# Attention's second product: four split fp32r products an image, or fp32 products of two images in four column groups

## The reference, cut to what matters

```
qkv = x @ qkv_w + qkv_b
attn = einsum('bqd,bkd->bqk', q * scale, k)
rel_h = einsum('bhwc,hkc->bhwk', q, Rh);  rel_w = einsum('bhwc,wkc->bhwk', q, Rw)
attn = softmax(attn + rel_h[..., :, None] + rel_w[..., None, :], axis=-1)
out = einsum('bqk,bkd->bqd', attn, v)
y = out @ proj_w + proj_b
```

## Time and profile before

| | |
|---|---|
| median of the runs | 1782.19 us |
| the profiled execution: its time, its span | 1781.53 us, 1779.3 us |
| PE busy, weight loads busy | 1477.8 us (83%), 1308.6 us |
| DVE, ACT, POOL busy | 1251.0, 899.5, 800.3 us |
| mean granted clock of TensorE | 0.798 |
| DMA, mean over the span | 92 GB/s |

### The profile page before, as it was taken

The page is one execution under the profiler, slowest core; times in us unless marked ns, Lnnn a source line. Parts: engine busy times, 40 slices in busy tenths (PEclk is TensorE's granted clock), DMA queues, the critical chain, the costliest instruction groups (busy, mean ns, idle before and its releaser), DMA issues. The chain is left out here.

```text
span 1779.3 us, 50706 instructions
## 1 busy us (share of the span) xinstructions
PE 1477.8 (83%) x19315; PEld 1308.6 (74%) x19315; DVE 1251.0 (70%) x4156; ACT 899.5 (51%) x1894; POOL 800.3 (45%) x888
## 2 busy tenths in 40 slices
PE   4868888888876886989976989899998697888977
PEld 4757777777765685878965667688884587787976
DVE  7877877877878656878856694544446646887874
ACT  3633333333345665767833433555553555666862
POOL 2812222222226054758952210556651415676974
PEclk9955555555558898999987589999995689999998
DMA  3000000000002585658415304333225458666812
GB/s 88 1 21 4 4 4 4 4 4 4 4 4 84 152 241 150 154 138 172 96 37 160 126 14 148 114 96 93 87 78 154 145 149 266 162 140 145 162 31 58
DMA packets 71882, 164.52 MB, mean 92 GB/s; under 512 B 17842, under 2 KB 43066, under 8 KB 69148
## 3 DMA queue, kind: packets, MB, share of 16 engines
q1 hardware_dynamic: 66268, 148.44, 31.6%
q0 software_dynamic: 5376, 12.85, 2.4%
HBM read 93.84 MB, written 67.42 MB: 91 GB/s over the span
## 5 line engine op out<-in xcount | busy, mean ns | idle before, releaser
L1065 POOL TENSOR_TENSOR l_arena<-l_arena,l_arena 98x784 fp32r<-98x784 f32 x192 | 360.5, 1881 | 136.5 <-ACT l_arena L1303 132.0
L514 PE MATMUL gru_ps_r<-gru_hp,gru_wp 128*128 128x16 f16 x3920 | 199.7, 176 | 68.3 <-DVE gru_hp L489 68.3
L514 PEld LDWEIGHTS gru_ps_r<-gru_hp,gru_wp 128*128 128x128 f16 x3920 | 150.4, 105 | 88.7 <-DVE gru_hp L489 88.7
L1300 ACT ACTIVATE l_arena<-l_ps 98x784 fp32r<-98x784 f32 x192 | 158.6, 826 | 103.7 <-PE l_ps L1154 101.7
L1375 DVE TENSOR_REDUCE l_mt<-l_ps 98x4 fp32r<-98x784 f32 x192 | 186.8, 973 | 27.4 <-PE l_ps L1133 22.9
L514 PE MATMUL gru_ps_n<-gru_hp,gru_wp 128*128 128x16 f16 x3920 | 191.2, 174 | 0.0
L567 POOL TENSOR_TENSOR gru_kept<-gru_keep,l0s_state 128x32 f32<-128x32 f32 x196 | 49.3, 252 | 305.9 <-ACT gru_keep L582 305.9
L1171 PE MATMUL l_ps<-l_arena,l_arena 128*66 128x196 f32 x768 | 162.7, 264 | 22.3 <-DVE l_arena L1343 20.7
L580 ACT ACTIVATE gru_reset<-gru_ps_r,gru_unscale 128x32 f32<-128x32 f32 x196 | 56.5, 288 | 216.9 <-PE gru_ps_r L514 216.9
L1172 PE MATMUL l_ps<-l_arena,l_arena 128*66 128x196 f32 x768 | 158.9, 259 | 0.0
L1303 ACT ACTIVATE l_arena<-l_ps 98x784 f32<-98x784 f32 x192 | 157.2, 819 | 0.0
(11 more groups left out here) (386 smaller groups left out, 4512.9 us busy)
## 6 DMA issues: line engine op xcount, KB each, us to landing
l_arena<-qk SPq DMA_DIRECT2D x96, 294.0 KB
qk<-l_arena SPq DMA_DIRECT2D x48, 392.0 KB, 6.0
rel<-l_arena SPq DMA_DIRECT2D x24, 686.0 KB
l_arena<-rel SPq DMA_DIRECT2D x48, 343.0 KB
qk<-l_arena SPq DMA_DIRECT2D x12, 784.0 KB, 10.5
l_arena<-in_experts_dram SPq DMA_DIRECT2D x8, 1152.0 KB, 7.5
l_arena<-x SPq DMA_DIRECT2D x24, 294.0 KB, 5.5
l_arena<-x SPq DMA_DIRECT2D x24, 196.0 KB, 4.2
```

What stands on the lines that cost most here:

```text
L514: last = pe.matmul(out[:, b, B * m:B * m + B], wp[:, wi, g, m, :], hp[:, b, part, B * k:B * k + B], start=False, stop=True, skip_group_che ...
L1065: pool.tensor_tensor(pl[g % LOWS][:TH, :, :], p32[:TH, g % 2, :, :], ph[:TH, g % 4, :, :].bitcast(f32), ALU.subtract).then_inc(pl_ready, 1)
L1300: act.activation(ph[:TH, g % 4, :, :], banks, ACT.Exp).then_inc(p_high, 1)
```

## The change

The probabilities stay fp32 and are not split: one exponential an image, into one of six buffers `probs`. The values stay fp32 as well, in a layout `v` with 17 columns a head, of which the last is one. Every second step, two images are weighed at once: eight fp32 products with 32 stationary columns each (16 values, the one, and 15 columns of what follows, which a zero row in `wo` drops later), each into 32 partitions of the bank O: image even or odd, head 0 or 1. The sum is the 17th row of each group. ACT copies the even image's 64 rows, DVE the odd one's, both into `o_quad`. SP stores the sums from there, eight images at a time, one row a head. POOL's subtraction, the splitting of values, `ring` and the padding fills go; the ones are filled into `v` by POOL ahead of the loop.

Two orders change beside that. ACT runs one image behind instead of two (step i handles image i - 1, before the copy and the `rel` of that step). The 14 `rel` steps of a quad are 1 to 8 and then every even step to 20 instead of 1 to 7 and 11 to 17, their two halves have a tile each, and on DVE `rel` comes ahead of the copy. The wait in ACT's `rel` is as it was.

```diff
-AT_QKA = AT_V + 2 * B * C
+VW = HEADS * (HD + 1)
+AT_QKA = AT_V + 2 * B * VW + 16
...
-    REL_STEPS = (1, 2, 3, 4, 5, 6, 7, 11, 12, 13, 14, 15, 16, 17)
+    REL_STEPS = (1, 2, 3, 4, 5, 6, 7, 8, 10, 12, 14, 16, 18, 20)
...
-    LOADS, SLOTS, LOWS = 3, 3, 3
+    LOADS, SLOTS = 3, 6
...
+        probs = [arena.place(at, 2, TB) for at in (0, 2 * TB, 4 * TB, 6 * TB, AT_W, AT_W + 2 * TB)]
+        rel_tiles = [arena.place(at, N, dt=f32r) for at in (2 * N, N)]
...
+        def kept_rows(g):
+            p, b = divmod(g, B)
+            row = 64 * (p % 2)
+            return o_quad[p // 2][row:row + 64, b * T:(b + 1) * T]
...
-                def store_sums(g):
...
+                def store_sums(h):
+                    p, half = divmod(h, 2)
+                    sp.wait_ge(even_kept, 4 * (h + 1))
+                    sp.wait_ge(odd_kept, 4 * (h + 1))
+                    cols = slice(half * N // 2, (half + 1) * N // 2)
+                    for head in range(2):
+                        row = 64 * (p % 2) + 32 * head + HD
+                        sp.dma_start(sums_dram[p, half, head:head + 1, :], o_quad[p // 2][row:row + 1, cols]).then_inc(sums_stored, 16)
...
-                    g = i - LAG - 1
-                    if g >= 0 and g % 2 == 1:
-                        store_sums(g)
+                    if i >= 12 and i % 8 == 4:
+                        store_sums((i - 12) // 8)
...
-                pool.memset(ph[CP:, :, :, :].bitcast(f32), 0.0).then_inc(ph_padded, 1)
...
+                pool.memset(v[:TH, :, :, HD:], 1.0).then_inc(ones_ready, 1)
+                pool.memset(v_flat[:TH, 2 * B * VW:], 0.0).then_inc(ones_ready, 1)
                 for g in range(IMAGES):
-                    pool.wait_ge(p_ready, g + 1)
-                    if g >= LOWS:
-                        pool.wait_ge(o_summed, g - LOWS + 1)
-                    pool.tensor_tensor(pl[g % LOWS][:TH, :, :], p32[:TH, g % 2, :, :], ph[:TH, g % 4, :, :].bitcast(f32),
-                                       ALU.subtract).then_inc(pl_ready, 1)
...
                 def weigh_values(g):
...
+                    p, b = divmod(g, B)
+                    pe.wait_ge(p_ready, g + 2)
+                    if g >= 2:
+                        pe.wait_ge(even_kept, g // 2)
+                        pe.wait_ge(odd_kept, g // 2)
+                    for keys in range(2):
+                        for odd in range(2):
+                            for head in range(2):
+                                row = 64 * odd + 32 * head
+                                place = (2 * (b + odd) + keys) * VW + (2 * p + head) * (HD + 1)
+                                last = pe.matmul(ps[row:row + 32, O_BANK, :T], v_flat[:TH, place:place + 32],
+                                                 probs[(g + odd) % SLOTS][:TH, head, keys * T:keys * T + T],
+                                                 start=keys == 0, stop=keys == 1, skip_group_check=True)
                     last.then_inc(o_summed, 1)
...
-                    if i >= LAG:
-                        weigh_values(i - LAG)
+                    if i > LAG and (i - LAG) % 2 == 1:
+                        weigh_values(i - LAG - 1)
...
+                def keep_even(g):
+                    act.wait_ge(o_summed, g // 2 + 1)
...
+                    act.activation(kept_rows(g), ps[:64, O_BANK, :T], ACT.Copy).then_inc(even_kept, 1)
+
+                for i in range(IMAGES + LAG):
+                    if 1 <= i <= IMAGES:
+                        g = i - 1
                         act.wait_ge(t_summed, g + 1)
...
+                        act.activation(probs[g % SLOTS][:TH, :, :], banks, ACT.Exp).then_inc(p_ready, 1)
+                    if i > LAG and (i - LAG) % 2 == 1:
+                        keep_even(i - LAG - 1)
                     if i in rel_of_step:
                         rel(rel_of_step[i])
...
+                def keep_odd(g):
+                    dve.wait_ge(o_summed, g // 2 + 1)
...
+                    dve.tensor_copy(kept_rows(g), ps[64:128, O_BANK, :T]).then_inc(odd_kept, 1)
...
-                    if i >= LAG:
-                        keep_products(i - LAG)
                     if i in rel_of_step:
                         rel(rel_of_step[i])
+                    if i > LAG and (i - LAG) % 2 == 1:
+                        keep_odd(i - LAG)
```

More of the change, by code:

```diff
@@ L767, in attention_layer @@
         k = arena.place(AT_K, 2, N, dt=f32r)
-        v = arena.place(AT_V, 2 * B, C)
+        v_flat = arena.place(AT_V, 2 * B * VW + 16)
+        v = v_flat[:, :2 * B * VW].rearrange("p (i h d) -> p i h d", i=2 * B, h=HEADS)
         qk_a, qk_b = arena.place(AT_QKA, 2, N, dt=f32r), arena.place(AT_QKB, 2, N, dt=f32r)
@@ L775, in attention_layer @@
         xy = arena.place(AT_QKA, CB, N)
-        ring = arena.place(AT_W, SLOTS, TB)[:2]
         at, tail = AT_Q, []
@@ L821, in attention_layer @@
         s_summed, max_ready = s.sem("s_summed"), s.sem("max_ready")
-        t_summed, p_high, p_ready, pl_ready = (s.sem(n) for n in "t_summed p_high p_ready pl_ready".split())
-        o_summed, o_kept, sums_kept, sums_free = s.sem("o_summed"), s.sem("o_kept"), s.sem("sums_kept"), [s.sem(f"sums{n}_free") for n in range(SLOTS)]
+        t_summed, p_ready = s.sem("t_summed"), s.sem("p_ready")
+        o_summed, even_kept, odd_kept, sums_stored = (s.sem(n) for n in "o_summed even_kept odd_kept sums_stored".split())
         extra_in = s.sem("extra_in")
@@ L834, in rel_tile @@
             quad, j = divmod(r, REL)
-            return (rel_h0, rel_w0)[j // 7] if quad == 0 else rel_tiles
+            return (rel_h0, rel_w0)[j // 7] if quad == 0 else rel_tiles[j // 7]
         def rel_out(r, low):
@@ L939, in load @@
                     sp.dma_start(dst[row:row + rows, :, cols].bitcast(f32), src[:, :, cols].bitcast(f32)).then_inc(quarter_in[part], 16)
-                def store_sums(g):
[L942 to L945, removed]
+                def store_sums(h):
[6 more added lines that the diff above has]
+                        sp.dma_start(sums_dram[p, half, head:head + 1, :], o_quad[p // 2][row:row + 1, cols]).then_inc(sums_stored, 16)
                 def load_sums(h):
-                    for slot in range(SLOTS):
-                        sp.wait_ge(sums_free[slot], 16 * ((B // 4 * (h + 1) - slot + SLOTS - 1) // SLOTS))
+                    sp.wait_ge(sums_stored, 32 * (h + 1))
                     if h:
@@ L1036, in _ @@
                 pool.wait_ge(ident_ready, 1)
[L1037 to L1041, removed]
                 pool.wait_ge(rel_stored, 64)
@@ L1158, in weigh_values @@
                 def weigh_values(g):
[L1159 to L1165, removed]
-                    out = ps[:66, O_BANK, :T]
-                    for head in range(2):
-                        for keys in range(2):
-                            cols = slice(keys * T, keys * T + T)
-                            values = vs[:, 2 * (g % 8) + keys, head, :]
-                            pe.matmul(out, values, ph[:, g % 4, head, cols], start=head == 0 and keys == 0, stop=False)
-                            last = pe.matmul(out, values, pl[g % LOWS][:, head, cols], start=False, stop=head == 1 and keys == 1)
+                    p, b = divmod(g, B)
[11 more added lines that the diff above has]
+                                                 start=keys == 0, stop=keys == 1, skip_group_check=True)
                     last.then_inc(o_summed, 1)
@@ L1251, in value @@
                     act.wait_ge(v_summed, i + 1)
-                    act.activation(v[:TH, i, :], ps[:TH, V_BANK + i % 2, :C], ACT.Copy).then_inc(v_ready, 1)
+                    act.activation(v[:TH, i, :, :HD], ps[:TH, V_BANK + i % 2, :C].rearrange("p (h d) -> p h d", h=HEADS), ACT.Copy).then_inc(v_ready, 1)
                 def rel(r):
@@ L1362, in _ @@
                 last_order(item, lambda i: None)
-                def lower_values(n, head):
-                    dve.wait_ge(vh_ready, 2 * n + head + 1)
-                    dve.tensor_tensor(value_parts(n, head, 1), values_of(n, head), value_parts(n, head, 0).bitcast(f32), ALU.subtract).then_inc(vl_ready, 1)
-                for n in range(2):
-                    for head in range(2):
-                        lower_values(n, head)
                 for i in range(IMAGES + LAG):
```

67 lines of the change are left out of this document (13 added, 54 removed).

## The result

The changed kernel takes 1836.16 us, the median of four runs (1832.58 to 1837.30); the kernel before took 1784.82 us beside it. The ratio is 1.028 [1.025, 1.031]: slower by 51 us, where 48 were forecast. The profiled execution took 1837.30 us, its span 1834.8 us.

A forecast was written before the change was run, and what follows sets the result against it. Plain steps were bound by POOL with PE just under, early thirds by the `rel` chain; loops +44, loop ends -6, clock +10 us gave +48 on 1781.5, so 1830 us; own range 1810 to 1855, 8 in 10 range 1766 to 1902.

The forecast's parts named there:

- W: Time of the eight new fp32 products, 16 records, every second step: 1.47 us, between 0.65 and 2.61 us.
- first eight steps of the thirds: First seven `rel` steps of a third: 3.65 us each, plus W and about 0.3 us where there is `weigh`.
- rest of a third: Plain steps left in a third after the `rel` steps: ten, at a mean of 2.12 us.
- nine record times: In `weigh`, a product's second record at best lies beside the next product's first, giving W = 1.47 us.
- my lower bound: In `weigh`, four column groups really run at once: W = 0.65 us, total 1774 us; rival's chance 0.33.
- a drain: Around `weigh`, 0.16 us of tail exposed twice per image pair: W = 1.79 us, total 1848 us; chance 0.10.
- two rivals: For `weigh`: four groups at once (W = 0.65, chance 0.33) and a drain at entry and exit (0.32 us more, chance 0.10).
- ACT's order: In `rel` steps, ACT's eviction stands behind that step's exponential, holding the next `rel`: 3.65 us a step, before 3.12.
- The stall at the eighth `rel`: At step 8, ACT's eighth eviction waits until the first seven are stored: 8.95 us from store issue to release.
- The second half's pairs: The later `rel` steps, on even steps: a chain through ACT, DVE and query logits of 6.17 us per two steps.
- The clock: In `rel` steps without `weigh`, a third at clock 0.50 adds about 10 us, ends 0 and 25.
- I see no new DMA wait: On SP's queue, the load behind the second `rel` store, issued at step 21, has over 20 us until step 32.

The follow-up runs named there:

- the run with the old steps: Changed kernel with `rel` back in steps 1 to 7 and 11 to 17 of a third: 1854.17 us, 1.042.
- both edits: Changed kernel with ACT's `rel` ahead of the exponential and its wait for the `rel` store put back by one half: 1706.69 us, 0.959.
- The added work on PE: Changed kernel with the four query logits products of the first seven `rel` steps of a third made three times: 1821.81 us, 1.024.

## Why the prediction was right, and where it was not

The time was right (1836 against 1830), and the loops were to take 552.6 us with the clock's 10 and took 554.4. But this comes of errors of both signs, about 30 us each; that they cancel to within 6 us is luck.

| step of the prediction | predicted | measured |
|---|---|---|
| W | 1.47 us | 0.98 us |
| pair of plain steps | 4.23 us | 3.75 us |
| last third, 31 steps | 65.6 us | 58.0 us |
| first eight steps of the thirds | 30.5 and 34.1 us | 34 and 37 us |
| steps 8 to 21, eighth `rel` and the six after it | 49.3 us | 49.6 to 51.0 us |
| rest of a third | ten steps, 21.2 us | eleven steps, 21.6 to 27.7 us |
| end of the loop, both layers | -6 us | -5.5 us |

- **W is the term that was mis-sized**, 0.98 us against 1.47 and outside the 1.3 to 1.65 of the forecast's own range. The step that failed is "products start in program order", from which the "nine record times" came. I had written that the forecast is wrong if four records start together; they do. Four groups run at once in either order, so my lower bound holds for the records themselves (bunches 0.17 us apart), and about the 0.32 us that I had priced as a drain come on top: 0.65 + 0.32 = 0.97, against 0.98. So two rivals that I had weighed as alternatives came in together; that the 0.32 us are a drain is argued and not shown. With 31.5 W a layer this is 31 us less than I forecast.
- The Trainium skill's rule that groups run concurrently ("TensorE: Matmul & The Clock Gate", "Part 3: Packing small matmuls") agrees with the trace: four starts within 40 ns. Its second half, that products start and end in program order, does not agree, and the measurement decides: with the two products of a group next to each other the starts are still in fours. I had joined this half to the first to argue against it.
- Its drain at a change of tiling mode ("TensorEngine Tiling (Array Packing)", Key Properties) fits the 0.31 us of idle weight load behind the 16 records, with four groups as with one; since the operands' type changes there too, the trace does not prove it.
- **ACT's order** was right in mechanism and size: 3.64 us for 3.65, and putting `rel` first is worth 78 to 85 us, with what the clock gives back in it.
- **The stall at the eighth `rel`** was right: 8.84 us for 8.95 from store to release, in all four thirds a step of 10.4 us, and some 20 us went with the wait.
- **The second half's pairs**: 6.3 us for 6.17.
- **The clock** was put at +10 us (0 to 25); filling PE's gap in the first eight steps took 12 us off the loops. The price was about right. I had put it on the steps without a `weigh`; in the first eight steps it fell mostly on those with one, which are 6.3 to 7.0 us long at the lower clock and 4.84 from `rel` to `rel` at the higher.
- **A count was wrong.** From the eighth `rel` to the maximum of step 21 there are 13 steps, so eleven plain steps remain in a third and not ten: 4 x 1.9 = 7.5 us too few.
- **"I see no new DMA wait" was wrong.** DVE's inverse waits for the load of the sums, 5.55 us near step 57 of the first layer and 2.47 us in the second. Of the 16.3 us of such waits 9.4 lie inside the loops; the 5.7 us of before all lie behind their ends. In the first layer's second third the rest takes 27.7 us for it. That sums are stored eight images at a time is not enough to make this wait: the run with the old steps stores them in the same way, and there DVE waits for them behind the loops alone (6.4 us). The traces show one difference on SP's queue: the second `rel` store was issued 10.1 us before it there (843.09 and 853.21) and 6.7 us before it in the changed kernel (837.60 and 844.30). I had looked only at the loads of queries behind that store. With both edits and `rel` in steps 1 to 14 a wait of 6.4 us was there too, so which transfer holds the load up stays open.

Together: -31 for W, against +7.5 for the count, about +13 for the waits in the rest of the thirds, +3 in the second halves, and +9 in the first eight steps: these took 19 us more than the chains with W = 0.98, of which I had put 10 down to the clock. The added work on PE removes 13 of the 19. Of the other 6, 2.9 are that added work itself, in the first step of each third, where PE has no gap for it (in three of the four 2.4 us instead of 1.7), and some 1.5 are only a matter of counting: DVE's copy of about 0.4 us stands ahead of the maximum that ends each of the four stretches. Under 2 us stay unexplained. Had I only had W right, I would have forecast 1799 us: right sign, wrong size.

## What to carry to other kernels

When an edit shortens the work of idle engines, look first at where it puts what remains in the order of each queue: one eviction moved behind an exponential cost some 80 us (the clock's part in it), more than four times what all 106 plain steps gave (2.04 - 1.88 us each, 17 us). Weigh two rivals that act on the same term also as a sum, since both can be true. And a bank or tile that was split in two brings nothing until the wait that guarded the one is rewritten.

## What the runs showed of the hardware that I had not expected

- Records in different column groups ran side by side: 16 fp32 records of 196 columns took 0.80 us to the next product in four groups and 2.77 us in one, and of two program orders between the groups neither changed the starts in fours, 0.17 us apart.
- Going from fp32r products to fp32 products of 32 columns and back cost about 0.3 us a time, with one group in use (2.96 us by the step's length, against 16 x 0.166 = 2.65) as with four (0.98 against 0.65).
- Work thrown away can save time: 56 records more in a stretch of 34 us brought the granted clock from 0.74 to 1.00 and the stretch to 30.4 us, with PE's busy time the same (22 us).
